# Per-block sums of a graph attention layer: stored four blocks at a time, four to a DRAM row

## The reference

```
for l in range(L):
    xn = _layernorm(h, ln1_g[l], ln1_b[l])
    q, k, v = (xn @ w[l] + b[l]).reshape(n, H, DH) for each of wq, wk, wv
    scores = jnp.einsum('ehd,ehd->eh', q[dst], k[src]) * scale
    m = jax.ops.segment_max(scores, dst, num_segments=n)
    ex = jnp.exp(scores - m[dst])
    z = jax.ops.segment_sum(ex, dst, num_segments=n)
    agg = jax.ops.segment_sum((ex / z[dst])[:, :, None] * v[src], dst, num_segments=n)
    h = h + agg.reshape(n, TD) @ wo[l] + bo[l]
    xn2 = _layernorm(h, ln2_g[l], ln2_b[l])
    h = h + jax.nn.gelu(xn2 @ w1[l] + b1[l], approximate=False) @ w2[l] + b2[l]
```

## Time and profile before

| | |
|---|---|
| median of 3 runs | 3874.39 us (3865.78 to 3884.16) |
| profiled execution, its own time | 3841.41 us |
| its span | 3839.6 us, 37354 instructions |
| busy share: PE, DVE, ACT, POOL | 59%, 65%, 35%, 48% |
| granted TensorE clock, mean | 0.734 of full speed |
| DMA | 623.31 MB, mean 162 GB/s |

### The profile page before, as it was taken

One profiled execution on the slowest core, in us unless ns is written; L12 is line 12 of the kernel. 1 busy time (PEld: TensorE's weight loads), 2 busy tenths in 40 slices (PEclk: granted clock), 3 DMA queues, 4 the chain that ended last, 5 costly groups with the idle time before them and its releaser, 6 DMA issues. The chain is left out here.

```text
span 3839.6 us, 37354 instructions
## 1 busy us (share of the span) xinstructions
PE 2269.0 (59%) x7207; PEld 1535.9 (40%) x7208; DVE 2484.9 (65%) x3957; ACT 1328.0 (35%) x3895; POOL 1842.5 (48%) x1938
## 2 busy tenths in 40 slices
PE   5634555555455555588854555555555555487898
PEld 3412333333333333365632333333333333365676
DVE  5766776777677787534435877776777777644333
ACT  1213443444344344222213444443444444222131
POOL 4055666666666666111036666666666666111000
PEclk8866666666676676699976766666766766689899
DMA  3365777777767766321246777776776767322101
GB/s 102 113 177 164 210 210 206 210 208 206 209 205 210 212 203 202 95 69 60 76 132 191 211 210 210 211 209 202 212 208 200 213 196 211 97 61 61 47 31 34
DMA packets 293455, 623.31 MB, mean 162 GB/s; under 512 B 52005, under 2 KB 163805, under 8 KB 293284
## 3 DMA queue, kind: packets, MB, share of 16 engines
q0 software_dynamic: 149904, 471.38, 42.2%
q1 hardware_dynamic: 143380, 150.27, 12.3%
HBM read 526.62 MB, written 94.78 MB: 162 GB/s over the span
## 5 line engine op out<-in xcount | busy, mean ns | idle before, releaser
L746 POOL DMA_INDIRECT ring<-kv_table,stage_ix x1760 | 1679.9, 954 | 994.9 <-issue 542.6
L992 PE MATMUL bank<-qs,hot_q 128*128 x1760 | 722.6, 559 | 678.6 <-issue 350.6
L1005 PE MATMUL bank<-ring,hot_w 128*128 128x272 f32 x1760 | 694.0, 533 | 489.4 <-issue 289.0
L1902 DVE TENSOR_TENSOR ring<-ring,bank 128x1024 f32<-128x1024 f32 x440 | 532.3, 1210 | 571.9 <-issue 362.2
L992 PEld LDWEIGHTS bank<-qs,hot_q 128*128 128x128 f32 x1760 | 466.2, 277 | 859.6 <-issue 761.0
L1005 PEld LDWEIGHTS bank<-ring,hot_w 128*128 128x128 f32 x1760 | 414.4, 255 | 754.5 <-issue 497.9
L1907 DVE TENSOR_REDUCE s<-ring 128x32 f32<-128x1024 f32 x440 | 532.5, 1210 | 4.2
L1245 ACT ACTIVATE stage_o<-bank 128x272 f32<-128x272 f32 x440 | 167.6, 386 | 515.7 <-remote 299.5
L1230 ACT ACTIVATE s<-bank 128x8 f32<-128x8 f32 x440 | 78.0, 177 | 720.2 <-remote 398.7
L1220 ACT ACTIVATE hot_q<-pos_b,row_of 128x128 f32<-128x128 bf16 x880 | 303.8, 394 | 11.7 <-DMA pos_b<-rel_d 8.7
L1919 DVE TENSOR_TENSOR bank<-ring,bank 128x512 f32<-128x512 f32 x440 | 300.5, 683 | 0.0
(11 more groups left out here) (317 smaller groups left out, 2151.0 us busy)
## 6 DMA issues: line engine op xcount, KB each, us to landing
agg_d<-stage_o SPq DMA_DIRECT2D x440, 136.0 KB
ring<-kv_table,stage_ix POOLq DMA_INDIRECT x1760
pos_b<-rel_d SPq DMA_DIRECT2D x54, 256.0 KB
kv_table<-ring SPq DMA_DIRECT2D x50, 250.0 KB
h_dram<-ring SPq DMA_DIRECT2D x15, 625.0 KB
ring<-h_dram SPq DMA_DIRECT2D x15, 625.0 KB
ring<-in_x_dram SPq DMA_DIRECT2D x10, 625.0 KB
ring<-kv_table SPq DMA_DIRECT2D x10, 625.0 KB
```

Of the source, the lines that this page charges most:

```text
L746: gps.indirect_dma_start(out=chunk[:, par * G + i, j, :], out_offset=None, in_=table, in_offset=bass.IndirectOffsetOnAxis(ap=stage_ix[:, p ...
L992: mm = ten.matmul(q_bank(third, i)[:, 0:QC], hot_q[:, i % 4, a * P:(a + 1) * P], qs[:, bass.ds(t * QC + a * QC, QC)], start=(a == 0), stop ...
L1005: mm = ten.matmul(b_acc[i % 2][:, lo - OWN:MC], hot_w[:, i % 4, :], chunk[:, s, j, lo:ROW], start=(j == 0), stop=(j == QD // 2 - 1), skip_ ...
L1902: tt(k_, k_, q, ALU.mult).then_inc(S["q_used"], 1)
```

## The change

`agg_d` is laid out anew: position p of the four blocks 4g to 4g + 3 lies in four neighbouring rows, g * 512 + p * 4 + (0 to 3), so one position has 4352 contiguous bytes. `stage_o` has two halves of four block buffers (eight in all); SP stores one half with one DMA. The last four blocks of a layer go in two stores of two blocks each. ACT waits for a half's store before the first of its four evacuations only. `firsts` is four DMAs, since a block's last position now lies in groups of four. The three index tables are rewritten to the new rows by five integer operations each time (`rows_packed`), once for `get_ix` and `put_ix` together and once for `home_ix`. The first half's semaphore counts one store per group, the second's starts 16 ahead.

```diff
-                def put(b, i):
-
-                    hold(sp, S["evac"], b + layer * NB + 1, S["sp_passed"])
-                    sp.dma_start(agg_d[bass.ds(b * P, P), :], stage_o[:, i % 4, :]).then_inc(S[f"agg_out{i % 4}"], 16)
+                def put(k, q):
+
+                    hold(sp, S["evac"], k * G + ((q + 1) * QB + layer * NB), S["sp_passed"])
+                    rows = agg_d[bass.ds(k * (G * P) + q * (QB * P), QB * P), :]
+                    sp.dma_start(rows.rearrange("(p b) c -> p b c", b=QB), stage_o[:, q, :, :]).then_inc(S[f"agg_out{q}"], 16)
+
+                def put_pair(k, i):
+
+                    hold(sp, S["evac"], k * G + (i * 2 + 2 + layer * NB), S["sp_passed"])
+                    rows = agg_d[k * (G * P):k * (G * P) + QB * P, :].rearrange("(p b) c -> p b c", b=QB)
+                    sp.dma_start(rows[:, i * 2:i * 2 + 2, :], stage_o[:, 0, i * 2:i * 2 + 2, :]).then_inc(S[f"agg_out{2 + i}"], 16)
...
                     if not first:
-                        for i in range(G - 4, G):
-                            put((k - 1) * G + i, i)
-                    for i in range(4):
-                        put(k * G + i, i)
+                        put(k - 1, 1)
+                    if nn:
+                        put(k, 0)
+                    else:
+                        for i in range(2):
+                            put_pair(k, i)
...
-                sp.dma_start(l_first, agg_d[0:NB * P, :].rearrange("(a b e) c -> b a e c", a=2, e=P)[:, :, P - 1, :]).then_inc(S["l_in"], 16)
+                last = agg_d[0:NB * P, :].rearrange("(g p b) c -> g p b c", p=P, b=QB)[:, P - 1, :, :]
+                for a in range(2):
+                    for b0, b1 in cuts_of[a]:
+                        if (b1 - b0) % QB:
+                            rows = last[b0 // QB, b0 % QB:b0 % QB + (b1 - b0), :]
+                        else:
+                            rows = last[b0 // QB:b1 // QB, :, :]
+                        sp.dma_start(l_first[b0 - a * HB:b1 - a * HB, a, :], rows).then_inc(S["l_in"], 16)
...
-                    if not fresh:
-                        hold(act, S[f"agg_out{i % 4}"], k * (G // 4 * 16) + (layer * (NB // 4) + i // 4) * 16, S["act_passed"])
+                    q = i // QB
+                    if i % QB == 0 and (q or not fresh):
+                        hold(act, S[f"agg_out{q}"], k * 16 + stored(q, layer), S["act_passed"])
                     act.wait_ge(S["agg"], n + 1)
-                    sca.activation(stage_o[:, i % 4, :], b_acc[i % 2][:, 0:MC], ACT.Copy).then_inc(S["evac"], 1)
+                    sca.activation(stage_o[:, q, i % QB, :], b_acc[i % 2][:, 0:MC], ACT.Copy).then_inc(S["evac"], 1)
...
+            def rows_packed(x, pos, at):
+
+                do(ts(pos, x, P - 1, 2, ALU.bitwise_and, ALU.logical_shift_left))
+                do(ts(at, x, 7, QB - 1, ALU.logical_shift_right, ALU.bitwise_and))
+                do(ts(x, x, 9, 9, ALU.logical_shift_right, ALU.logical_shift_left))
+                do(tt(x, x, pos, ALU.bitwise_or))
+                do(tt(x, x, at, ALU.bitwise_or))
+
             def columns_of_blocks():
                 v.wait_ge(S["prep_pe"], 8)
                 st.did(vec.tensor_copy(e_rel, rows_at))
-                for n, dst in enumerate((contn_col, get_ix, put_ix)):
-                    st.did(vec.tensor_copy(dst[:, :], bank[3][0:HB, n * 2 * H:(n + 1) * 2 * H].rearrange("p (a h) -> p a h", a=2)[:, :, 0]))
-                st.sync(v)
+                st.did(vec.tensor_copy(contn_col[:, :], bank[3][0:HB, 0:2 * H].rearrange("p (a h) -> p a h", a=2)[:, :, 0]))
+                do(vec.tensor_copy(link_ix[:, :, :], bank[3][0:HB, 2 * H:6 * H].rearrange("p (n a h) -> p n a h", n=2, a=2)[:, :, :, 0]))
+                rows_packed(link_ix[:, :, :].rearrange("p n a -> p (n a)"), e_t0[0:HB, 0:4].bitcast(U32), e_t1[0:HB, 0:4].bitcast(U32))
                 v.sem_inc(S["pens_made"], 1)
...
                     do(vec.tensor_copy(home_ix[:, :], hb))
+                    rows_packed(home_ix[:, :], hb.bitcast(U32), bn.bitcast(U32))
```

More of the change, by code:

```diff
@@ L60 @@
 RING = SLOTS * QD * ROW
+QB = 4
+STORES = NB // G
+assert G == 2 * QB and NB == STORES * G + QB
 PAIRS = (NGRP - 4) // 2
@@ L69, in uses, with stored @@
     return len(range(slot, NB, SLOTS))
+def stored(i, layers):
+    return 16 * (layers * STORES + 1 if i == 1 else layers * (STORES if i == 0 else 1))
 def hold(eng, sem, value, passed):
@@ L179, in program @@
         q_tab = scratch("q_tab", [QT * P, QC])
-        agg_d = scratch("agg_d", [NB * P + NB, MC])
+        agg_d = scratch("agg_d", [NB * P + QB * P, MC])
         h_dram = scratch("h_dram", [N, D])
@@ L193, in program @@
         contn_col = sb("contn_col", [HB, 2])
-        get_ix = sb("get_ix", [HB, 2], U32)
-        put_ix = sb("put_ix", [HB, 2], U32)
+        link_ix = sb("link_ix", [HB, 2, 2], U32)
+        get_ix, put_ix = link_ix[:, 0, :], link_ix[:, 1, :]
         home_ix = sb("home_ix", [TN, NT], U32)
@@ L207, in program @@
         mtab = sb("mtab", [G * H, 2, NGRP])
-        stage_o = sb("stage_o", [P, 4, MC])
+        stage_o = sb("stage_o", [P, 2, QB, MC])
         up_bias = sb("up_bias", [P, FFN // P])
@@ L604, in _ @@
             kv_in, kv_out = kv_table, kv_table2
+            cuts_of = (((0, HB // QB * QB), (HB // QB * QB, HB)), ((HB, HB + 2), (HB + 2, NB)))
+            assert HB % QB == 2
             def firsts(layer):
                 for i in range(4):
-                    sp.wait_ge(S[f"agg_out{i}"], (layer + 1) * (NB // 4) * 16)
-                sp.dma_start(l_first, agg_d[0:NB * P, :].rearrange("(a b e) c -> b a e c", a=2, e=P)[:, :, P - 1, :]).then_inc(S["l_in"], 16)
+                    sp.wait_ge(S[f"agg_out{i}"], stored(i, layer + 1))
+                last = agg_d[0:NB * P, :].rearrange("(g p b) c -> g p b c", p=P, b=QB)[:, P - 1, :, :]
[6 more added lines that the diff above has]
+                        sp.dma_start(l_first[b0 - a * HB:b1 - a * HB, a, :], rows).then_inc(S["l_in"], 16)
             sp.wait_ge(S["edges_over"], 1)
@@ L758, in links @@
                 for i in range(4):
-                    pool.wait_ge(S[f"agg_out{i}"], (layer + 1) * (NB // 4) * 16)
+                    pool.wait_ge(S[f"agg_out{i}"], stored(i, layer + 1))
                 for a in range(2):
@@ L2007, in links @@
                 ls.sync(v)
-                v.wait_ge(S["l_in"], (layer + 1) * 16)
+                v.wait_ge(S["l_in"], (layer + 1) * 64)
                 for e, x in enumerate((l_first, l_home)):
```

3 lines of the change are left out of this document (2 added, 1 removed).

## The result

The changed kernel takes 3854.95 us in the median (3845.13 to 3867.7, 17 runs), the kernel before 3874.39 us beside it (3865.08 to 3888.1, 17 runs). The ratio is 0.9947, with a 95% interval of 0.9938 to 0.9957: 20 us faster, 0.53%. The prediction said no difference (3878 us). The measured time lies inside its range, but the change moved the time, and the terms of its sum had no gain in them.

The account below looks back on a forecast made before the run. The prediction took the edge stage as bound by POOL's issue rate, then by late `agg`. Its terms, 1.0 + 0.67 + 1.14 + 0.67 = +3.5 us, put 3874.4 us at 3878 us, range 3843 to 3906.

Parts of the forecast that it names:

- Stores in the edge stage: Edge stages: 112 stores in place of 440 and fewer ACT waits on `agg_out` save nothing; 0 us.
- about 47 us: Sign that the forecast is right: POOL's group of 32 gathers in the edge stage keeps this length.
- DMA load: Edge-stage stores: larger pieces might make DMA engines' work cheaper; saving bounded by 0 and 145 us, taken as 0.
- the rival at 3830 us: Edge stages: lighter DMA load shortens POOL's slot pauses, saving 48 us, a quarter of the stores' 193 us; chance 0.17.
- The latency of each store: Edge stages: ACT's evacuation waits are late stores; fewer would save 340 us, giving some 3540 us; chance 0.03.
- Opening, +1.0 us: Opening: five dependent index operations less one copy lengthen DVE's chain to the first gather by 1.0 us.
- End of layer 0, +1.8 us: End of layer 0: larger last store +0.67 us, and four `firsts` DMAs delaying the weights +1.14 us.
- end of layer 1, +0.67: End of layer 1: larger last store costs 0.67 us; the weights' delay is hidden by the home gather.
- Home gathers, 0 with a bound of +59: Ten heads: gathering rows 4352 bytes apart costs 0, at most 5.9 us at each, +59 us.
- the slow rival: Home gathers: rows four apart gather more slowly, 3.0 us at ten heads, giving 3908 us; chance 0.15.
- Packets: DMA queue q1: about 42,000 packets fewer, as a sign that the forecast is right.
- The base of the sum: Whole kernel: +3.5 us, found on the profiled execution of 3841.4 us, was added unchanged to the median 3874.4 us.

Follow-up runs that it names:

- chips A and C: Two chips of the follow-up runs, where the kernel before took 3864.88 and 3869.55 us (first) and 3878.78 us (second).
- batch 4: Four kernels against the kernel before on one chip (3878.78 us): old or new stores, each with `pens` at the old or new address; 3857.03 to 3881.02 us.
- copy of before: The kernel before, unchanged, run as one more program beside itself: 3871.18 us, ratio 1.0019, and on another chip 3881.02 us, ratio 1.0008.
- the kernel with a store per block: Changed kernel with its layout and eight buffers, but 440 single-block stores: 3862.23 us, ratio 0.9993 to before; on another chip 3836.34 us, 0.9995.
- doubled stores: Every store issued a second time to a table nobody reads: kernel before 3876.75 us, ratio 1.0010; changed kernel 3864.37 us, ratio 0.9982.
- old rows: Changed kernel's four-block stores and eight buffers, but the table keeps its old rows, in pieces of 1088 bytes: 3858.22 us, ratio 0.9980 to before.
- B: A chip of the follow-up runs: kernel before 3842.77 us, changed kernel 3845.74 us, ratio 1.0006.
- small stores: Changed kernel with 440 more stores of 16 rows each to a table nobody reads: 3836.26 us, ratio 0.9993 to before; on another chip 3837.49 us, 0.9986.
- SP's wakes without a transfer: Changed kernel, but SP waits for every block's evacuation and raises the semaphore itself: 3839.86 us, ratio 0.9994 to before.
- D: A chip of the follow-up runs where the kernel before took 3840.71 us; the changed kernel itself was not run there.

## Why the prediction was wrong

The step that failed is the term *Stores in the edge stage*: SP saves issues, "so this is worth nothing", and ACT drops waits, "so nothing again". On chips A and C the edge stages with 112 or 224 stores are shorter than those with 440 or more in every profile, and on C the stores are worth 14.5 to 18 us of the total. The reasoning excluded one mechanism, a late landing that holds ACT, and there it was right: in the changed profile 3 of 109 waits on `agg_out` took 0.7 us each, 2.2 us in sum, and the others 0.02. It then treated that as the only mechanism. The time is in the slot pauses, which the earlier trace rows and the window view had shown as the only place to win. Its signs were too coarse to see it there: in batch 4 a group of 32 gathers takes 47.7 us in the copy of before and 47.2 in the changed kernel, "about 47 us" in both, and half a microsecond in each of 51 groups is the 25 us. (Two slips in its numbers change nothing: 32 x 1.25 is 40.0, and three quarters of the way to 3830 is 3842.)

The premise that ACT's waits "let it through at once before" was not quite so, and what the traces show there was not followed up. ACT's register instructions (they prepare counters for its waits) take 0.04 us in the middle, but now and then one takes 0.7. (The counts are from the instruction records of the traces.) In the edge stages of batch 4 this happened 49 times (36.2 us) in the copy of before and 4 times (2.9 us) in the changed kernel. On A and C it is 44 to 50 times in each program where ACT waits for every block, and 1 to 13 times where it waits for every half (20 in the profile of before that the prediction read). 24 of the copy's 436 waits on `agg_out` took 0.2 to 1.4 us in place of 0.02, each 9 us or more after the last landing that their counter shows, so it is not a store that they waited for. ACT's evacuation stands ahead of `agg`, so these stops may be part of the pauses. They are not all of it: the kernel with a store per block had only 12 of them on A, 9.2 us, and edge stages of 2417.4 us. What causes them is open.

*DMA load.* The prediction bounded it by 0 and 145 us and took 0 from the price per kilobyte. That price fell a little: a piece of 4352 bytes took 179 to 184 ns in layer 0's edges on A and C (189 with doubled stores), one of 1088 bytes 48.2 to 48.7 in the kernels with 440 stores or more, so 5 to 8% less per byte. With the gathers, whose pieces became cheaper too, the mean busy time of the engines fell by 36 us on C and 41 on A, changed kernel against copy. But doubled bytes brought some 160 us of it and cost about 7 us, so the load as such has a small price, and the rival at 3830 us had the right sign by the wrong size. It is not shown to be the mechanism either: with old rows the small pieces stay and the gain stays.

*The latency of each store*, the rival at 3540 us, had 340 us for the 328 fewer stores. Even if all of the 14.5 to 18 us came from their number, that would be 0.05 us for each.

*Opening, +1.0 us.* The five operations cost about what was said: the first gather starts at 224.8 us in the mean of the 13 profiles that have them and at 223.5 in the 7 that don't, 1.3 us later, with ranges of 2 to 3 us in each. Whether that reaches the end is not shown, since POOL's first stop, which PE ends, comes behind it. The prediction had no term for the addresses, though the change names them: two tiles of 8 bytes became one. That gave back 4 to 7 us of the opening's step in the like pairs. The pieces of `pens` take 28.4 ns in the mean of the six profiles at the old address and 19.6 ns in that of the fourteen at the new one; the source did not move, only the side that is written. Yet most pieces cost the same at both: the middle one takes 18 to 25 ns at the old address and 18 at the new one. What grows is the share of slow ones, over 30 ns: 23 to 39% against 0 to 14%. The Trainium skill ("DMA: Bandwidth & Descriptors", How a descriptor splits into AXI transactions, with Why small descriptors are slow), which the prediction cited for the stores, says of reads that one which does not start at a multiple of 256 bytes needs bytes in front of it too. By its count of beats and cycles, an estimate, a 256-byte piece at 32 bytes past would cost 12 cycles in place of 11, 9% more. Carried over to the side that is written, it has the sign of the rows; the measured 45% decides the size. A beat more in every piece is not what the rows show, so why some pieces are slow stays open.

*End of layer 0, +1.8 us; end of layer 1, +0.67.* The rows of batch 4, copy of before and then the changed kernel (the first view's window cuts off PE's row):

```profile
1593.62 0.33 SPq L609 DMA_DIRECT2D ring<-agg_d  x1
...
1594.42 1.02 POOL L761 DMA_INDIRECT ring<-agg_d,get_ix  x1 [40.67 <-DMA agg_d<-stage_o]
...
1617.32 2.92 PE L842 MATMUL bank<-ring,g_col 128*125 128x512 f32 x3 [15.30 <-DMA g_col<-in_L_gnn_ln_b_dram]
```

```profile
1573.63 2.61 SPq L637 DMA_DIRECT2D ring<-agg_d  x4
...
1574.43 1.02 POOL L789 DMA_INDIRECT ring<-agg_d,link_ix  x1 [41.01 <-DMA agg_d<-stage_o]
...
1597.79 5.31 PE L870 MATMUL bank<-ring,g_col 128*125 128x512 f32 x8 [13.36 <-DMA g_col<-in_L_gnn_ln_b_dram]
```

POOL's wait behind the last gather grew by 0.34 us (said: 0.67). The four issues take 2.61 us in place of 0.33 (said: 1.14 more). PE starts 65.3 us after the layer's last gather in place of 64.5, 0.8 us for both terms together. Small, and the right sign. In the span such terms can't be told: what lies outside the edge stages takes 1435 to 1456 us in the twenty profiles.

*Home gathers, 0 with a bound of +59.* Right. The waits of all heads (us, times), copy of before and changed, batch 4:

```profile
  DMA ring<-h_dram: 149.6, 9
  DMA ring<-agg_d,stage_h: 10.6, 1
```

```profile
  DMA ring<-h_dram: 148.5, 9
  DMA ring<-agg_d,stage_h: 6.4, 1
```

Rows four apart did not make them later, so the slow rival has no footing here. *Packets*: 47210 fewer where about 42,000 were said; the sum left out the 4-byte pieces that come with each transfer.

*The base of the sum.* The prediction noted that the profiled execution was 0.85% faster than the median and below all three runs shown, and carried its terms over unchanged. That was a sign that profile and runs may not have come from the same conditions. On B, whose times that execution has, "no difference" is what the runs say: 1.0006 (0.9995 to 1.0017) for the changed kernel.

**What stays open.** Shown: on A and C the new stores shorten POOL's pauses, on C by 20 to 25 us in one profile each, and on B no gain can be told. Against a sole cause in the size of the pieces, in the bytes or in late landings at ACT speak the runs above. Which part of the new stores does it is not shown. Number of transfers or the eight buffers: one comparison on A (0.9980 with 112 old-row stores, 0.9993 with 440 new-row ones) favours the number, by less than a copy of before differs from itself, while its edge stages differ by 17 us, against a scatter of 10. The doubled and the small stores don't show a price per store; the small ones, and SP's wakes without a transfer, were never tried on a chip like A or C. ACT's stops of 0.7 us were not tested at all. What makes the edge stages of one program 25 us longer on one chip than on another (a store per block, A and D) was not found.

## What to carry to other kernels

Before a gain of a half per cent is explained, make sure that both profiles come from one chip: the same program differed by 38 us between chips here, twice the effect, and a change can pay on one and not on another. When a change touches the list of tiles, compute the new addresses: here a tile loaded in pieces of 256 bytes did better at a multiple of 256 bytes than 32 past one (no other offset was tried), and its load stood in front of the one that a stage waited for. An argument that rules out one way in which stores can hurt does not rule out the others; where all slack sits in one pause, keep a chance for anything that runs beside it.

## What the hardware showed beyond what was expected

- A shift of 32 bytes in the destination brings the mean cost of 256-byte pieces from 25.3 to 33.4 ns down to 18.1 to 22.5 ns (six profiles at the old address, fourteen at the new), by fewer slow pieces and not by a cheaper usual one.
- Register instructions of ACT that take 0.04 us as a rule take 0.7 us 44 to 50 times in the edge stages of the programs where ACT waits for every block on A and C, and at most 13 times where it waits for every fourth.
- The same program takes 3842.8 and 3840.7 us on two chips and 3864.9 to 3878.8 us on two others, at a granted clock of 0.73 to 0.74 throughout.
- A copy of the kernel before stood at 1.0019 (1.0004 to 1.0033) and 1.0008 (0.9993 to 1.0023) of it. Two tenths of a per cent are the floor of such a comparison, whatever its interval says.
- Pieces of the gathers, 4096 bytes, took 217 to 218 ns beside 112 stores and 221 to 222 ns beside 440 on A and C, and 209 ns beside 224 large ones. A cheaper piece and a shorter stage do not go together: with 440 stores they took 222 ns on D too, where the stage is 25 us shorter than on A.
